# Attention over 1500 keys on one NeuronCore: logits laid out with the rows on the partitions, or with the keys on them

## What is computed

```
h = layer_norm(x)
q = h @ wq + bq ;  k = ctx @ wk + bk ;  v = ctx @ wv + bv       # 16 heads of 128
k, v get one more row each: bias_k, bias_v
weights = softmax(q k^T / sqrt(128))                            # over 1501 keys
x = x + (weights v) @ wo + bo                                   # twice, then:
x = x + gelu(layer_norm(x) @ w_fc1 + b_fc1) @ w_fc2 + b_fc2
```

## Time and profile before

| | |
|---|---|
| median of 3 runs | 1407.51 us |
| the profiled execution, first to last instruction | 1409.6 us |
| attention, layer 1 and 2 | 67 to 622 us, 751 to 1309 us |
| TensorE busy | 1338.0 us, 95% |
| VectorE / ScalarE / POOL busy | 931.6 / 675.5 / 509.1 us |

### The profile page before, as it was taken

How to read it: one execution, slowest core, us unless ns; L and a number is a source line. 1 busy time by engine, 2 the same in 40 slices (tenths; PEclk the granted TensorE clock), 3 DMA queues, 4 the chain that set the end, 5 groups by cost and what they waited for, 6 DMA issues and landing times.

```text
span 1409.6 us, 26063 instructions
## 1 busy us (share of the span) xinstructions
PE 1338.0 (95%) x7504; PEld 1158.5 (82%) x7504; DVE 931.6 (66%) x1738; ACT 675.5 (48%) x1164; POOL 509.1 (36%) x465
## 2 busy tenths in 40 slices
PE   6999999999999999987698999999999999999887
PEld 4788888888888888876587888888888888888676
DVE  6766666666766666557685767676757576665664
ACT  5744444444444444457494444444444444444664
POOL 4633233332323232037572415141414141410682
PEclk9999999999999999999899999999999999999898
DMA  5402011111111110012251202020202020100221
GB/s 178 137 23 66 28 60 40 48 44 44 44 44 44 44 45 21 0 46 57 73 161 46 67 22 66 21 70 17 83 4 87 1 86 7 58 0 1 67 75 36
DMA packets 30413, 72.57 MB, mean 51 GB/s; under 512 B 3072, under 2 KB 4144, under 8 KB 30368
## 3 DMA queue, kind: packets, MB, share of 16 engines
q1 hardware_dynamic: 30368, 72.02, 17.0%
HBM read 71.53 MB, written 0.48 MB: 51 GB/s over the span
## 4 chain that ended last, share of the span: by engine, by line
PE 83%; DVE 4%; issue 4%; ACT 3%; POOL 2%; DMA 2%; DVEq 0%; ACTq 0%; SPq 0%; POOLq 0%
PE logits L554 33%; PE bank L565 22%; PE bank L567 11%; PE bank L547 10%; PE bank L518 2%; PE bank L575 2%; ACT oth L838 1%; DVE g_prod L1005 1%; POOL w L375 1%; PE logits L597 1%; DMA w_raw<-weights 1%; DMA nat_stage<-ctx_nat 1%; POOL pm L471 1%; ACT w L738 1%; DVE oth L1092 1%
## 5 line engine op out<-in xcount | busy, mean ns | idle before, releaser
L554 PE MATMUL logits<-ctx,qs 128*128 (+2 forms) x2016 | 540.7, 404 | 0.4 <-DVE qs L1047 0.4
L565 PE MATMUL bank<-ctx,pt 125*128 (+1 forms) x1344 | 478.1, 395 | 0.0
L554 PEld LDWEIGHTS logits<-ctx,qs 128*128 128x128 f32 x2016 | 355.8, 190 | 53.3 <-DVE qs L1047 0.7
L567 PE MATMUL bank<-ctx,pt 125*128 (+1 forms) x1344 | 378.4, 282 | 0.0
L811 ACT ACTIVATE pt<-bank 125x512 fp32r<-125x512 f32 x336 | 200.7, 597 | 263.3 <-PE bank L547 262.8
L565 PEld LDWEIGHTS bank<-ctx,pt 125*128 125x128 f32 x1344 | 252.6, 188 | 58.0
L1062 DVE TENSOR_TENSOR pt<-bank,pt 125x512 fp32r<-125x512 f32 x336 | 232.2, 691 | 71.1 <-ACT pt L811 68.8
L397 POOL CAST qs<-qt 128x256 fp32r (+1 forms) x110 | 43.8, 398 | 621.8 <-PE logits L554 621.8
L752 ACT ACTIVATE e<-logits,neg_max 128x1500 f32<-128x1500 f32 x110 | 166.7, 1515 | 200.2 <-DVE neg_max L955 200.2
L567 PEld LDWEIGHTS bank<-ctx,pt 125*128 125x128 f32 x1344 | 252.8, 188 | 2.9
L945 DVE TENSOR_REDUCE mx<-logits 128x1 f32<-128x512 f32 x336 | 227.9, 678 | 20.1 <-PE logits L554 7.8
(11 more groups left out here) (90 smaller groups left out, 1161.8 us busy)
## 6 DMA issues: line engine op xcount, KB each, us to landing
nat_stage<-ctx_nat SPq DMA_DIRECT2D x64, 375.0 KB
tr_stage<-ctx_tr SPq DMA_DIRECT2D x64, 375.0 KB, 5.1
w_raw<-weights SPq DMA_DIRECT2D x72, 256.0 KB, 2.7
dk_all<-dk_rows SPq DMA_DIRECT2D x2, 768.0 KB, 5.6
dk_all<-dk_rows SPq DMA_DIRECT2D x2, 256.0 KB, 3.8
xres<-x_rows SPq DMA_DIRECT2D x4, 112.0 KB, 2.3
out_rows<-xres SPq DMA_DIRECT2D x4, 112.0 KB, 1.9
bo<-out_bias SPq DMA_DIRECT2D x1, 336.0 KB, 3.8
```

What stands on the lines that cost most here:

```text
L554: last = mm(logits[:, lo:hi], qs[:, a, c, :], ctx_tr_part(slot, c, m, lo, hi), start=(c, a, m) == terms[0], stop=(c, a, m) == terms[-1])
L565: mm(O_BANK[:, 0:2 * D], pt[:, HI, g, j * P:(j + 1) * P], ctx_nat_tile(slot, t, 2 * D), start=(t == 0), stop=(t == NCT - 1), skip_group_ch ...
L567: last = mm(O_BANK[:, 0:D], pt[:, LO, g, j * P:(j + 1) * P], ctx_nat_tile(slot, t, D), start=False, stop=(t == NCT - 1), skip_group_check= ...
```

## The change

Logits are made with the keys on the partitions. A batch is cut into two groups of row tiles, of 4 (512 rows) and of 3 (384 rows). A group goes through the 12 key chunks one by one, so a batch has 24 steps, k = 0 to 23 (chunk c = k mod 12, h = 0 or 1), and step k of every engine does:

- PE: `score_chunk` k (six products, stationary 125 keys, moving 512 or 384 rows, one of two PSUM banks), then `group_contexts` of the step 16 back (per tile three products of 258, 256 and 258 columns; two columns of ones give the row sums).
- DVE: `shifted` for the step 14 back (subtract the rows' maximum), `chunk_max` k (running elementwise maximum).
- ACT: `weights_hi` for the step 14 back (exponential twice, to fp32r and to fp32), then copy of the logits of k out of PSUM into one of 12 slots.
- POOL: `weights_lo` for the step 14 back.

At c = 0 the running maximum is transposed (`max_transposes`, one per tile), reduced and met with `lb` on DVE (`group_max`); at c = 1 it is spread over partitions (`spread_max`, one transpose per tile). At c = 4 the finished group is normalized out of its four (three) output banks, at c = 5 and 6 its result is transposed in pairs of tiles. Both layers' exponential transposes are gone. `ctx` has one slot instead of two, and the order of its pieces is new on SP, DVE and POOL.

```diff
+GT = (4, 3)
+SUB_LAG, PV_LAG = 14, 16
+RING = 3
@@ SP
                 with sp.Fori(0, B - 1) as b:
                     for p in range(PIECES):
+                        load_tr(b + 1, l * (B * PIECES) + b * PIECES + PIECES + p, p)
+                    for p in range(PIECES):
                         load_nat(b + 1, l * (B * PIECES) + b * PIECES + PIECES + p, p)
-                        load_tr(b + 1, l * (B * PIECES) + b * PIECES + PIECES + p, p)
@@ PE
+            def score_chunk(h, c, k):
+                R = GT[h] * P
+                terms = [(half, a, m) for half in range(DC) for a, m in TERMS]
+                for half, a, m in terms:
+                    last = mm(scores(h, k), ctx_tr_chunk(half, a, c), qs[h][:, m, half, 0:R],
...
+            def weighted_context(h, c, j):
+                hi, lo = (pt[:, a, c % RING, j * P:(j + 1) * P] for a in (HI, LO))
+                mm(O_BANK[j][:, 0:D + 2], hi, ctx_nat_hi(c), start=(c == 0), stop=False, skip_group_check=True)
+                mm(O_BANK[j][:, 0:D], hi, ctx_nat_lo(c), start=False, stop=False, skip_group_check=True)
+                return mm(O_BANK[j][:, 0:D + 2], lo, ctx_nat_hi(c), start=False, stop=(c == NCT - 1),
...
+                    if c == 0:
+                        at = l * (2 * GROUPS) + b * 4 + (i // NCT) * 2
+                        pe.wait_ge(on_act, INIT + at)
+                        pe.wait_ge(on_dve, INIT + l * (3 * B) + b * 3 + (i // STEPS) * 3 + 2 * h)
...
+                    pe.wait_ge(pt_lo, INIT + l * LAYER_STEPS + b * STEPS + (i + 1))
...
+                    if pair == 0:
...
+                    else:
+                        pe.wait_ge(ot_out, INIT + done + 1)
...
+                            pe.wait_ge(copied, INIT + l * LAYER_STEPS + b * STEPS + (k - 1))
+                            if c == 0 and not (first and h == 0):
+                                pe.wait_ge(qs_lo, INIT + l * (2 * GROUPS - 2) + b * 4 + 2 * h)
...
+                            score_chunk(h, c, k)
+                        if c == 0 and (h == 1 or not first) and k < NCT + (0 if tail else 1):
+                            pe.wait_ge(max_done, INIT + group * (NCT - 1))
...
+                            max_transposes(1 - h)
+                        if c == 1 and (h == 1 or not first) and k < NCT + (0 if tail else 2):
+                            pe.wait_ge(max_ready, INIT + group)
+                            pe.wait_ge(sub_done, INIT + (group - 1) * NCT)
+                            spread_max(1 - h)
+                        i, ph, pc = lagging(k, PV_LAG)
+                        if i >= 0 or not first:
+                            group_contexts(b, i, ph, pc)
@@ ACT
+                def weights_hi(b, i, h, c):
+                    act.wait_ge(sub_done, INIT + l * LAYER_STEPS + b * STEPS + (i + 1))
+                    act.wait_ge(pv_mm, INIT + l * LAYER_STEPS + b * STEPS + (i + 1 - RING))
+                    go(split_weights(h, HI, c), slot(h, c), ACT.Exp)
+                    go(slot(h, c), slot(h, c), ACT.Exp).then_inc(exp_done, 1)
...
+                            go(slot(h, c), scores(h, k), ACT.Copy).then_inc(copied, 1)
...
+                        if c in (6, 7) and not first and not (tail and h == 1):
+                            transposed_context(b - 1, h, c - 6)
@@ DVE
+                        if c == 4 and not first:
+                            normalized(b - 1, h)
+                        i, ph, pc = lagging(k, SUB_LAG)
+                        if (i >= 0 or not first) and not (tail and i >= 0):
+                            shifted(b, i, ph, pc)
+                        if c >= 1 and not tail:
+                            chunk_max(b, k, h, c)
+                        if c == 0 and (h == 1 or not first) and not (tail and h == 1):
+                            group_max(b - 1 if h == 0 else b, 1 - h)
+                        if k == 0 and not first and not tail:
+                            tr_part_hi(pieces + 3, 3)
+                        if k in (7, 10, NCT + 1, NCT + 4) and not first and not tail:
...
+                            nat_part_hi(pieces + p, p)
+                        if k in (NCT + 3, NCT + 6, NCT + 9) and not last:
+                            p = (k - NCT) // 3 - 1
+                            tr_part_hi(pieces + PIECES + p, p)
```

More of the change, by code:

```diff
@@ L138, in build @@
[L138 to L148, removed]
+        N_TR, N_NAT = DC * 2 * T, NCT * NAT_W
+        ctx = sb("ctx", [P, N_TR + N_NAT], F32R)
@@ L155, in build @@
+        place_at[0] = at_qs
+        oth = [sb(f"oth{s}", [P, 2, DC, ROWS], F32R) for s in range(2)]
+        assert place_at[0] <= at_max
+        place_at[0] = at_qs
+        g32 = [sb(f"g32_{s}", [P, ROWS], F32) for s in range(2)]
+        place_at[0] = at_max
         xn = sb("xn", [RGP, RG, D], F32)
@@ L180, in build @@
         hprod = sb("hprod", [H, LAYERS, K], F32)
[L183 to L187, removed]
+        psum = stack.enter_context(nc.psum_tensor("psum", [P, 8 * BANK], F32))
+        bank = [psum[:, i * BANK:(i + 1) * BANK] for i in range(8)]
+        S_BANK = [bank[0], bank[1]]
+        O_BANK = [bank[2 + j] for j in range(GT[0])]
+        NB_BANK, MT_BANK, OT_BANK = bank[6], bank[7], bank[7]
+        PICK_BANK = bank[6]
         LN_BANK = [bank[6], bank[7]]
@@ new lines, in _ @@
+                batch_steps(0, True, False)
+                with pool.Fori(1, B - 1) as b:
+                    batch_steps(b, False, False)
+                batch_steps(B - 1, False, True)
+                for k in range(SUB_LAG):
+                    i, h, c = lagging(k, SUB_LAG)
+                    weights_lo(B, i, h, c)
+                    if k in (7, 9, 11, 13):
+                        u = (k - 7) // 2
+                        weight_lo(l * JOBS + (H + u), u)
+                pool.wait_ge(pv_mm, INIT + (l + 1) * LAYER_STEPS)
@@ L571, in context_transposes @@
-            def context_transposes(n):
-                pe.wait_ge(on_ready, INIT + n + 1)
-                pe.wait_ge(ot_out, INIT + n)
-                for c in range(DC):
-                    last = nc.tensor.transpose(OT_BANK[:, c * P:(c + 1) * P], on[:, c * P:(c + 1) * P], ident[:])
+            def score_chunk(h, c, k):
[3 more added lines that the diff above has]
+                    last = mm(scores(h, k), ctx_tr_chunk(half, a, c), qs[h][:, m, half, 0:R],
+                              start=(half, a, m) == terms[0], stop=(half, a, m) == terms[-1])
+                last.then_inc(s_mm, 1)
@@ new lines, in max_transposes, with spread_max @@
+            def max_transposes(h):
+                for j in range(GT[h]):
+                    last = nc.tensor.transpose(MT_BANK[:, j * CT:(j + 1) * CT], t_max[h][:, j * P:(j + 1) * P],
+                                               ident[0:CT, 0:CT])
+                last.then_inc(mt_mm, 1)
+            def spread_max(h):
+                for j in range(GT[h]):
+                    last = nc.tensor.transpose(NB_BANK[0:CT, j * P:(j + 1) * P],
+                                               mx_group[:, j:j + 1].to_broadcast([P, CT]), ident[:])
+                last.then_inc(nb_mm, 1)
@@ L576, in context_transposes @@
+            def context_transposes(j0, j1, out_bank):
+                n = j1 - j0
+                for half in range(DC):
+                    for j in range(j0, j1):
+                        at = (half * n + (j - j0)) * P
+                        last = nc.tensor.transpose(out_bank[:, at:at + P], on[:, j, half * P:(half + 1) * P], ident[:])
                 last.then_inc(ot_mm, 1)
@@ L659, in _ @@
                 query_quad(QUADS - 1, True)
-                tiles = l * NT
                 pe.wait_ge(consts_in, 16 * N_CONSTS)
@@ L847, in _ @@
                     context_hi(s, s, l * H)
-                for u in range(2, 4):
-                    weight_hi(l * JOBS + (H + u), u, l * 8 + 4)
                 for u in range(2):
```

531 lines of the change are left out of this document (268 added, 263 removed).

## The result

The changed kernel takes 1504.14 us (1500.42 to 1507.68), against 1407.8 for the kernel before beside it: ratio 1.0663, 95% interval 1.0640 to 1.0686, or +96 us. The profiled execution has a span of 1502.3 us.

A forecast was written before the change was run, and what follows sets the result against it. PE's own work was taken as the bound. Per batch 62.2 us plus 4.8 of short waits; with filling, emptying, long waits of 6.0 us, 20 us of clock and 4 less for the heads: 1476 us (+68), range 1365 to 1535.

The forecast's parts named there:

- The long wait: At k = 16, T0's late load holds DVE's drain: PE waits 4.8 us more, POOL adds 1.2, in 12 batches.
- the drain's own part: At k = 16, PE waits 0.9 us for the output banks to be drained, apart from any late load.
- PE's own work: Scores, contexts and small transposes on PE: 62.2 us a batch against 68.9 before, 6.7 us to be won.
- The short waits: PE waits in every batch for drains, result transposes and the spread maximum: together 4.8 us a batch.
- The wait for the spread maximum: At k = 1 and 13, DVE's small operations held by POOL: 1.4 us a batch taken, between 0 and 2.9.
- the lock that the prediction tells of: SBUF lock held for a whole instruction: a full weights_lo before each of three DVE operations, 2.9 us, sum 21 us higher.
- The clock: PE's clock falls to half for 3.4 us at each of 12 holes, 1.7 us each: 20 us, ends 0 and 40.
- Filling and emptying: Pipeline 16 steps deep: batch 0 of a layer takes 47 us, the contexts at the end 29 us.
- The heads: After the attention, the heads start with four weights ready: 2 us less a layer, between 0 and 4.
- Rival 1: T0's load lands in time, long wait and clock loss go: 1384 us, or 1317 with short waits hidden; chance 0.28.
- Rival 2: POOL becomes the bound, weights_lo at 1.65 us between k = 15 and 23: +46 us, 1522 us; chance 0.17.
- Rival 3: Matmul time saved is eaten by weight loads, products 0.14 us apart instead of 0.119: +80 us in all; chance 0.05.

The follow-up runs named there:

- Experiment 1: Changed kernel with SP issuing T0 of the next batch right behind T1 to T3 and N0, no longer behind N3; 1410.89 us, ratio 0.9999.
- Experiment 2: Changed kernel, its load order kept, with each natural piece loaded in two transfers (partitions 0 to 111, 112 to 124); 1447.72 us, ratio 1.0257.
- the fastest kernel: Changed kernel with T0 loaded earlier, split natural loads, early result copy, output banks waited for singly, queries split at k = 12 and 14; 1345.80 us, ratio 0.9544.
- experiment 5: Changed kernel with ACT's copy of the first pair of result transposes moved before the exponentials at c = 6; 1483.26 us, ratio 1.0515.
- the kernel with 40 products: Changed kernel, its load order kept, with 40 unused products on PE before the context of step 16 in batches 1 to 7; 1488.31 us, ratio 1.0546.
- experiment 3: Changed kernel with both T0 issued ahead of the later natural pieces and natural pieces loaded in two transfers; 1404.21 us, ratio 0.9953.

## Why the prediction held, point by point

**The long wait** was right in place, in order and in who holds whom: T0 behind N3, DVE held at the cast, the drain behind it, PE behind the drain, once a batch. Experiment 1 removes it by the order alone and takes 93 of the 96 us with it. The wait with the drain's own part was put at 4.8 + 0.9 = 5.7 us and measured 7.0; less the 0.9, 6.1 lies within the 3.4 to 6.3 that were given. What mis-sized it is the landing. Two loads behind one another were put at 4.7 to 6.6 us, from rows with both kinds of load in flight and from 3.2 us for one alone; from N3's issue (236.06) to T0's landing (DVE's wait ends at 242.66) it is 6.6. And N2 was taken to be there when DVE came to it, but a natural piece takes 5.2 us, and DVE waited 1.71 for it. Experiment 2 shows the share of the natural loads in the whole: 57 us.

**PE's own work**, 62.2 us a batch, is 63.6 in the fastest kernel. The products of 258 columns start 0.12 apart as taken (timeline of the changed kernel):

```profile
233.28 0.28 PE L620 MATMUL psum<-ctx,pt 125*128 125x258 f32 x1
233.40 0.28 PE L621 MATMUL psum<-ctx,pt 125*128 125x256 f32 x1
233.52 0.28 PE L622 MATMUL psum<-ctx,pt 125*128 125x258 f32 x1
```

Scores of four tiles with the three tiles of `group_contexts` behind them are 2.48 to 2.59 us apart in the fastest kernel's steps without other work, where 2.47 were reckoned, since six products of 512 columns last 1.39 to 1.53 us instead of 1.40. The rest of the 1.4 us a batch was not traced. Over 14 batches the whole is 20 us.

**The short waits**: drains 0.6 at k = 4 (0.55 taken), the transposes 1.2 by the profile, 1.5 by the whole time of experiment 5 and 2.0 to 2.4 by its batches 7 (1.9 taken), the queries 1.1 (1.2 taken). The wait for the spread maximum (1.4 taken, between 0 and 2.9) hardly came, 0.2 us in one of the eight places. The difference that I feared (L1143, two SBUF operands) never overlapped a POOL operation. The maximum before it (L1140) did in 14 of its 32 cases, all of them at k = 12, and each time it ended with POOL's operation (two rows of the changed kernel's timeline, then durations in ns, min/median/max):

```profile
227.62 2.14 POOL L466 TENSOR_TENSOR pt<-slots,pt 125x384 fp32r<-125x384 f32 x2
229.34 0.44 DVE L1140 TENSOR_TENSOR mx_group<-mx_part,lb 128x4 f32<-128x4 f32 x1
...
L1140 DVE TENSOR_TENSOR mx_group<-mx_part,lb x32: 160/163/737, 90.3 to 1373.0; 128x4 f32<-128x4 f32 x16, 128x3 f32<-128x3 f32 x16
L1143 DVE TENSOR_TENSOR p_extra<-lb,mx_group x32: 160/163/166, 90.5 to 1373.2; 128x3 f32 x12, 128x4 f32 x12, 128x4 f32<-128x4 f32 x4, 128x3 f32<-128x3 f32 x4
```

POOL's second operation ends at 229.76 and the maximum at 229.78. It meets only the last part of a `weights_lo`, takes 0.37 to 0.74 us instead of 0.16, and its cover swallows the difference. So the lock that the prediction tells of is seen, but not a full `weights_lo` before each of the three: in this term that rule would have led further off than the middle I took, and zero would have been best. That the rule's 21 us would have brought the sum nearer to 1504 is luck. The cast of a transposed piece (L1030) did stretch, to a median of 0.95 us.

**The clock**: a fall behind each hole was foreseen, and 1.7 us each. The trace gives 2.2 on average over the 12 (1.9 in the hole shown), and the kernel with 40 products 1.8.

**Filling and emptying**: batch 0 takes 47.7 us (47 foreseen), the end of a layer's attention 30.6 (29), batch 7, without hole or queries, 65.4 (67.0). The heads do not start earlier for their four ready weights: from the end of one attention to the next it is 129.3 us against 128.7, where 2 us less a layer were taken.

Together: the attention is 602 and 604 us in the two layers where 591 was forecast, 555 before. That the sum came within 28 us is in part luck: PE's own work was taken 20 us too low and the wait for the spread maximum 20 too high. What the forecast was short by is then above all the hole, 12 x 1.3 = 16 us, the clock, 12 x 0.5 = 6, and the heads, 4. **Rival 1** (load in time) names the right lever: with the load in time experiment 1 gives 1411, not the 1384 that it was put at. Its batches 1 to 6 take 68.5 to 69.4 us instead of 67.0; the natural loads are 6.5 us of the difference (experiment 3), and the rest lies with PE's own work and the smaller terms. **Rival 2** (POOL the bound) is refuted as the cause of the loss, by experiment 1, and right about the next bound: once the hole and the short waits were gone, POOL's place for the queries was worth 29 us. **Rival 3** is refuted by the starts 0.12 apart, shown above.

## What to carry to other kernels

A count of columns says what a change can win, and the order of waits says what it does win: write down, for each wait on an in-order engine, what stands behind it, also on the queue that issues the loads. Here one slot of context instead of two made every load urgent (no run gives the changed kernel two slots), and the demand order (T0 before N3) was not the issue order; correcting that was worth 93 us with not one operation changed. When the largest hole is closed, look again, because waits that were small or covered (the queries' low part) then set the pace.

## What the runs showed of the hardware

- A load of 375 KB into 125 partitions landed 5.2 us after its issue at 101 to 135 GB/s with the DMA engines 25 to 33% busy. The same bytes as 112 and 13 partitions had moved 3.1 us after their issue. In the kernel before only the transposed loads had been timed; the profile's page gives no landing for the natural ones, and that is where the forecast's error began.
- Of the 6.8 us at half clock around a hole of 6.9 us, 3.0 lay inside the hole and cost nothing; over 12 such holes 39 of 92 us. With products for 5.0 us in the hole there was still a spell of 3.4 us at half clock behind 7 of the 12; with products for 7.1 us, none in the attention.
- A VectorE maximum of two small SBUF operands, 0.16 us when alone, took 0.37 to 0.74 us in the 14 of 32 cases in which a POOL operation was under way, and ended with that operation each time.
